# One product of 512 columns for the gradients of both W2 in the memory loop

## The reference

```python
def step(carry, x_t):                      # 16 steps, one for each row t
    params, mom = carry                    # two layers (W1, W2) for each image
    k = _l2norm(x_t @ Wk); v = x_t @ Wv
    lr, forget, eta = ...                  # one number each for an image
    g = grad_fn(params, k, v)              # of mean((mlp(params, k) - v) ** 2)
    new_mom    = eta * mom - lr * g
    new_params = params * (1 - forget) + new_mom
```

## Time and profile before

| | |
|---|---|
| median of 3 runs | 546.06 us (545.37 to 549.56) |
| the profiled execution: its own time | 546.64 us |
| its span in the trace | 544.8 us |
| TensorE busy | 476.3 us (87%) |
| TensorE weight loads busy | 295.2 us (54%) |
| VectorE, ScalarE, GpSimd busy | 293.7, 224.3, 99.8 us |

### The profile page before, as it was taken

How to read it: one execution, slowest core, us unless ns; L and a number is a source line. 1 busy time by engine, 2 the same in 40 slices (tenths; PEclk the granted TensorE clock), 3 DMA queues, 4 the chain that set the end, 5 groups by cost and what they waited for, 6 DMA issues and landing times.

```text
span 544.8 us, 11175 instructions
## 1 busy us (share of the span) xinstructions
PE 476.3 (87%) x3945; PEld 295.2 (54%) x3952; DVE 293.7 (54%) x1382; ACT 224.3 (41%) x1118; POOL 99.8 (18%) x101
## 2 busy tenths in 40 slices
PE   7899999999999998988887999778888887888886
PEld 4588888888865234855543776333333333333333
DVE  2966666666666756056556444664444444444443
ACT  2365556555525741025533344333333333333332
POOL 4287777767510000000000000000000000000000
PEclk8999999999997999999999999999999999999999
DMA  7600000000000000000000000000000000000000
GB/s 223 271 0 2 2 1 0 2 1 2 0 2 0 1 2 0 1 1 2 2 2 1 1 2 1 2 1 1 2 1 2 1 0 2 2 1 2 2 2 19
DMA packets 3081, 7.68 MB, mean 14 GB/s; under 512 B 1484, under 2 KB 2065, under 8 KB 2833
## 3 DMA queue, kind: packets, MB, share of 16 engines
q1 hardware_dynamic: 3026, 6.97, 3.8%
HBM read 6.71 MB, written 0.26 MB: 13 GB/s over the span
## 4 chain that ended last, share of the span: by engine, by line
PE 54%; DVE 22%; ACT 16%; issue 8%; DMA 0%; DVEq 0%; ACTq 0%
PE bk L700 12%; DVE bk L1491 8%; ACT gi L1050 6%; DVE mem L1494 6%; ACT bk L1054 6%; PE bk L659 6%; PE bk L340 3%; PE bk L585 2%; PE bk L508 2%; PE bk L838 2%; PE bk L603 2%; PE bk L489 2%; PE bk L467 2%; PE bk L477 2%; PE bk L392 2%
## 5 line engine op out<-in xcount | busy, mean ns | idle before, releaser
L838 PE MATMUL bk<-idle 128*64 128x512 bf16 (+1 forms) x650 | 175.7, 371 | 0.0
L700 PEld LDWEIGHTS bk<-mem,lvh 65*64 65x64 f32 x1536 | 79.9, 136 | 144.3 <-DVE mem L1494 142.5
L700 PE MATMUL bk<-mem,lvh 65*64 65x4 f32 x1536 | 102.1, 205 | 45.5 <-DVE mem L1494 45.1
L1050 ACT ACTIVATE gi<-bk 128x4 f32<-128x4 f32 x256 | 44.9, 175 | 136.7 <-PE bk L700 136.3
L1491 DVE TENSOR_TENSOR_SCAN bk<-gi 64x12 f32<-64x12 f32 x256 | 47.6, 186 | 91.1 <-ACT gi L1050 88.7
L1494 DVE SCALAR_TENSOR_TENSOR mem<-og,bk 64x4 f32<-64x4 f32 x256 | 38.5, 150 | 53.7 <-ACT bk L1054 53.7
L838 PEld LDWEIGHTS bk<-idle 128*64 128x64 bf16 x650 | 55.3, 110 | 16.1 <-issue 2.4
L1054 ACT ACTIVATE bk<-bk 64x4 f32<-64x4 f32 x256 | 36.6, 143 | 45.2 <-DVE bk L1491 45.2
L1498 DVE SCALAR_TENSOR_TENSOR gi<-mem,bk 64x4 f32<-64x4 f32 x255 | 39.1, 153 | 8.8
L1052 ACT ACTIVATE og<-bk 64x4 f32<-64x4 f32 x256 | 42.6, 167 | 0.0
L1140 DVE TENSOR_TENSOR mem<-mem,bk 128x256 f32<-128x256 f32 x64 | 27.0, 421 | 17.2 <-PE bk L385 11.4
(11 more groups left out here) (317 smaller groups left out, 743.7 us busy)
## 6 DMA issues: line engine op xcount, KB each, us to landing
cw<-in_cw SPq DMA_DIRECT2D x1, 3456.0 KB, 12.2
w<-in_w SPq DMA_DIRECT2D x1, 520.0 KB
mem<-in_memw SPq DMA_DIRECT2D x1, 512.0 KB, 3.6
w1g<-in_w1g SPq DMA_DIRECT2D x1, 512.0 KB
w<-in_w SPq DMA_DIRECT2D x1, 512.0 KB
xm<-in_xm SPq DMA_DIRECT2D x1, 256.0 KB, 2.7
xs<-in_x SPq DMA_DIRECT2D x1, 256.0 KB, 3.9
out<-xs SPq DMA_DIRECT2D x1, 256.0 KB, 2.0
```

What stands on the lines that cost most here:

```text
L700: return nc.tensor.matmul(bk[row:row + D, 2 * (s // CH % 2) + k, c:c + B], lvh[:, g, :], hist[:, s, :], start=False, stop=True, skip_group ...
L838: nc.tensor.matmul(bk[64:128, 1, 0:n], idle[:, 0:D], idle[:, 128:128 + n], start=True, stop=True)
L1050: nc.scalar.activation(gi[:, 2:2 + 3 * B:3], bk[:, bank, cols], ACT.Tanh).then_inc(sem("in_gate"), 1)
```

## The change

Both products that have `gtok` as the stationary operand become one of 512 columns, at the place of the later one. For that `dtokP` and `dh1tokP` lie side by side: `dh1tokP` gets one place between both parities of `dtokP`, so that in even steps `dtokP` stands left of it and in odd steps right of it. The result fills bank 4; which half belongs to which layer changes with the parity (`lo`). DVE waits for the one signal `dw2` and then updates L2A ahead of L2B. The buffer cleared at the start grows from 2816 to 3072 columns, and `dh1tokP` no longer has memory of its own.

```diff
-        pads = big[:, 5120:7936].rearrange("p (n c) -> p n c", c=128)
+        pads = big[:, 5120:8192].rearrange("p (n c) -> p n c", c=128)
...
-        dtokP = [pads[:, 16 + 2 * n:18 + 2 * n, :] for n in range(2)]
-        da0tok = [pads[:, 20 + n, :] for n in range(2)]
+        dtokP = [pads[:, 16 + 4 * n:18 + 4 * n, :] for n in range(2)]
+        dh1tokP = pads[:, 18:20, :]
+        both = [pads[:, 16 + 2 * n:20 + 2 * n, :] for n in range(2)]
+        da0tok = [pads[:, 22 + n, :] for n in range(2)]
...
-        dh1tokP = sb("dh1tokP", [128, 2, 128])
...
                 pe.wait_ge(sem("gtok"), t + 1)
                 pe.wait_ge(sem("dtok"), t + 1)
-                nc.tensor.matmul(bk[:, 4, 256:512], gtok[:, :], dtokP[par].rearrange("p a c -> p (a c)"), start=True,
-                                 stop=True).then_inc(sem("dw21"), 1)
...
                 pe.wait_ge(sem("dh1tok"), t + 1)
-                nc.tensor.matmul(bk[:, 6, 0:256], gtok[:, :], dh1tokP[:, :, :].rearrange("p a c -> p (a c)"), start=True,
-                                 stop=True).then_inc(sem("dw20"), 1)
+                nc.tensor.matmul(bk[:, 4, :], gtok[:, :], both[par].rearrange("p a c -> p (a c)"), start=True,
+                                 stop=True).then_inc(sem("dw2"), 1)
...
+                lo = 256 if (w, t % 2) in ((L2A, 1), (L2B, 0)) else 0
...
                     dve.wait_ge(sem("Q2"), t)
-                    dve.wait_ge(sem("dw21"), t)
-                    new_weights(t, L2B, "p21")
-                    dve.wait_ge(sem("dw20"), t)
+                    dve.wait_ge(sem("dw2"), t)
                     new_weights(t, L2A, "p20")
+                    new_weights(t, L2B, "p21")
```

More of the change, by code:

```diff
@@ L1134, in masked @@
                 return nc.vector.tensor_tensor(dst, src.rearrange("p (a c) -> p a c", a=2), mj, ALU.mult)
-            from_bank, lo = (4, 6, 5, 6), (256, 0, 0, 0)
+            from_bank = (4, 4, 5, 6)
             def new_weights(t, w, signal):
-                return nc.vector.tensor_tensor(Ps[t % 2][:, w, :], Q[:, w, :], bk[:, from_bank[w], lo[w]:lo[w] + 256],
+                lo = 256 if (w, t % 2) in ((L2A, 1), (L2B, 0)) else 0
+                return nc.vector.tensor_tensor(Ps[t % 2][:, w, :], Q[:, w, :], bk[:, from_bank[w], lo:lo + 256],
                                                ALU.add).then_inc(sem(signal), 1)
@@ L1151, in _ @@
                     dve.wait_ge(sem("Q2"), t)
-                    dve.wait_ge(sem("dw21"), t)
+                    dve.wait_ge(sem("dw2"), t)
+                    new_weights(t, L2A, "p20")
                     new_weights(t, L2B, "p21")
-                    dve.wait_ge(sem("dw20"), t)
-                    new_weights(t, L2A, "p20")
                     dve.wait_ge(sem("Q1"), t)
@@ L1223, in _ @@
             dve.wait_ge(sem("Q2"), T)
-            dve.wait_ge(sem("dw21"), T)
+            dve.wait_ge(sem("dw2"), T)
+            new_weights(T, L2A, "p20")
             new_weights(T, L2B, "p21")
-            dve.wait_ge(sem("dw20"), T)
-            new_weights(T, L2A, "p20")
             dve.wait_ge(sem("Q1"), T)
```

## The result

| | before | with the change |
|---|---|---|
| median of 5 runs | 546.06 us | 555.40 us (554.07 to 559.05) |
| ratio | | 1.0173, 95% interval 1.0141 to 1.0206 |
| forecast | | 553.0 us, range 550.7 to 556.5 |
| profiled execution: span | 544.8 us | 553.6 us |

The change made the kernel slower, as forecast, and the time lies in the range, 2.4 us above the forecast. The interval of the ratio makes the loss 7.7 to 11.2 us; 6.9 were forecast. Wherever kernels are compared here, executions more than 1.5% above the fastest one of the same kernel are left out.

What follows compares the result with a forecast made beforehand. The prediction took the loop as bound by TensorE's chain of small f32 products, 7.62 us a step. It added 16 x 0.43 = 6.9 us to the median 546.06, all other terms nothing: 553.0 us, range 550.7 to 556.5.

Steps and rivals of the forecast that it cites:

- The price and the place of the columns: L508's two passes each get 256 more columns behind the wait for dh1tok: 0.43 us a step, 6.9 us over 16.
- Merging is worth nothing: In the joined product, cost goes by columns: 0.215 us a pass for 256, 0.43 for 512, no gain from size.
- the rival in which the loads bind: TensorE's weight loads set the loop's pace; two fewer save 0.34 us a step, 5.4 us, giving 540.7; chance 0.03.
- L496's removal at nothing: L496 runs under DVE's making of dh1T, so taking it out of the step was counted as no gain.
- the bound of 0.10: Most that removing L496 could gain: 0.10 us a step between L501's load and its first transpose.
- Updates and POOL: W2 updates on DVE start later with 0.4 us of slack; POOL's wait grows from 1.89 to 2.3 us, hidden.
- The clock: Half-clock stretches, in the pause before L501 or behind the loop: up to 1.7 us each; several in the loop, chance 0.04.
- the three signs of being wrong: L490 to the copy under 1.46 us; a wait at L425 for DVE's update; granted clock below 1.00 in the loop.
- Its clue for the clock: Behind the loop, where TensorE had waited for DVE, a stretch of 3.3 us was granted half clock.

Runs made afterwards that it cites:

- the cover in place: Changed kernel with the old 256-column product run once more at L496's old place, as pure extra work: median 553.69 us, ratio 1.0124.
- the unmerged pair at the late place: Kernel before with L496 alone moved to L508's place, behind the wait for dh1tok, as a product of its own: median 554.62 us, ratio 1.0161.
- the one without the gradient: Changed kernel with L496's work gone (gradient of layer 1's W2 left out) and nothing in its place: 13 runs, 548.02 to 604.72 us, median 574.93.

## Why the prediction was right, and what it missed

- **The price and the place of the columns: right.** 0.43 us a step was forecast, and 7.62 became 8.05 with the cover in place; the unmerged pair at the late place took 8.08, merged 8.07. This part of the loss is the forecast's 6.9 us.
- **Merging is worth nothing: right.** The sum by rows held to 0.01 us a step; the loads that were saved (the rival in which the loads bind) were hidden.
- **L496's removal at nothing: nearly.** L496 held the transposes by 0.04 us, inside the bound of 0.10, and its absence lets three waits stand in a row, which cost 0.06. Net 0.02 a step, 0.3 us in all: 8.07, not 8.05. The three waits stood in the listed order of the change and were not priced.
- **Updates and POOL: right.** L425 does not wait (0.3 us of slack where 0.4 was forecast), and POOL's wait grew to 2.34 us (forecast 2.3).
- **What the sum put at nothing: the clock in the emptied wait.** The prediction asked only what L496's place costs when it is emptied, not what TensorE's work there keeps up. "The clock" stood among the rivals with this pause as a place and up to 1.7 us for a stretch, but it was kept out of the sum. In the profiled executions all five kernels with full work and the wait left empty show one or two stretches at half clock within the loop, and the one without the gradient shows half clock for twelve steps; the four with the wait filled show none. One such stretch cost 1.35 us in the changed kernel: 6.9 + 0.3 + 1.35 = 8.55 us, inside the measured 7.7 to 11.2. Of the three signs of being wrong this one came, a granted clock below 1.00 in the loop; the other two did not (L490 to the copy took 1.49 us, not less than 1.46, and L425 did not wait).
- **Its clue for the clock was misread.** The stretch at 165.0 was put down to TensorE having waited for DVE. That wait, 0.34 us, ends at 165.58, inside the stretch; in the microsecond ahead of it (163.9 to 164.9, granted 1.00) TensorE was busy for 0.92:

```profile
165.58 1.92 PE L557 MATMUL bk<-consts,xn 128*64 128x128 f32 x8 [0.34 <-DVE xn L1098]
```

- **Luck.** The range held the extra time because its high end, taken from the spread of the runs before, has room for two stretches; no row said how many this pause would bring, and several had a chance of 0.04. With the same pause the kernel without the gradient took up to 604.72 us.
- **Left open:** why the clock comes back after one stretch in one kernel and not in another, and the 1.45 us more behind the loop and 1.2 less ahead of it, which go with the stretches at half clock there. The kernel before itself took 543.9 to 552.0 us in the runs beside the experiments, with mean clocks from 0.993 to 0.973, so such stretches come and go without the change.

## What to carry to other kernels

Merging two f32 products with the same stationary operand gained 0.01 us a step here and lost the wait that one of them had filled, 0.43 us; price the columns by where they run, by the distance between starts. Before taking work out of a wait on TensorE, ask what the granted clock does without it, and leave an empty product there if need be. What can be gained around a wait is found by looking for work that is ready ahead of it: 0.24 us a step for L515 here, with no arithmetic changed.

## What the runs showed of the hardware that was not expected

- In the kernel without the gradient a wait of 0.43 us between TensorE's loads, 0.27 between its matmuls, stood in each step of 7.65 us, and after three steps the granted clock fell from 1.00 to 0.50 for the remaining 140 us of the loop; the step grew by half, to 11.74 us. Four empty bf16 products in that wait (0.44 us) kept it at 1.00, with steps of 7.62. With this wait left empty the five kernels with full work ran one or two stretches of some 3.3 us at half clock.
- A weight load that stands behind three waits started 0.115 us after the last signal's instruction ended, and one behind one wait (or with the others met at an earlier instruction) after 0.053. In the first case the trace holds a semaphore instruction of 0.05 us between the two.
- From 256 to 512 columns the two passes of an f32 product took time in proportion at full clock: 0.215 us each for 256, 0.43 for 512 (L507's second pass at 65.34, the next product at 65.77).
